# Four tiles' logits and gates turned by one transpose each, and bias products on bands of 32 rows

## The chip, the cores and the metric

The kernel runs on one core of one Trainium2 chip. The metric is the device time of one execution in microseconds (us), as the median over runs. The tensor engine is called PE, the vector engine DVE, the scalar engine ACT, GpSimd POOL, and the engine that issues most of the transfers SP.

## The reference

Two layers over `x` of 8 batches x 256 time steps x 256 channels. Layer 0 is a decayed scan followed by a mixture of eight gated experts with a router; layer 1 is a gated linear attention followed by a top-2 choice among eight 256x256 experts, with a bias for each. Two pieces matter here. Both routers multiply every token (row of x) by a 256x8 matrix to get eight logits for that token. And layer 1 adds, for every token, the two chosen experts' bias rows weighted by their gates:

```
logits = x @ gate_w.T                       # [tokens, 8]
gates  = softmax over the best two of 8
out    = sum over the two e: gates[e] * (x @ expert_w[e] + expert_b[e])
```

## The kernel before

The 2048 tokens are worked on in four groups (`GROUPS`) of 512, each of four tiles of 128 tokens (`TILES = 4`). Every matrix product is made in three passes of rounded operands (high by high, high by low, low by high; `passes`, L706). Group g's layer-1 work is laid between the layer-0 work of group g+1. Each engine runs a program of its own, in the order in which the functions are called in its `group` function; semaphores tie them together. The order of each engine is written out by hand.

**Logits.** `router_start` makes the logits of 512 tokens with the token along the free dimension: a PSUM bank of 16 rows (8 high parts, 8 low parts) by 512 columns. ACT (`logits_out`, L1078 is its copy helper) copies 16x512 to SBUF in one instruction, into `logitT`, a part of `weighted[1]`. `router_end` (L740 to L745) then turns it tile by tile: four transposes of 16x128, into 16 columns each. DVE reads the 64 columns (`route_start` for layer 0, `gates_start` for layer 1). There are two of these per group. On PE, layer 0's `router_end` stands right behind `transpose_y` of the group before, and layer 1's between the products r and k of `project_rkv`.

**Gates and bias.** `spread_gates` (DVE) writes the gates of a tile three times, at columns 0, 32 and 64 of 96 (`BIAS_K`), high and low parts. `transpose_gates` (L924) turns four tiles with four transposes of 128x96 into one bank; ACT (`gates_out`) copies 96x512 out as `gatesT`. `project_o` begins each tile's output product with `gatesT[:, cols]` times `bias_w` of 96 rows (L938) and goes on with six passes of the attention's output matrix in the same accumulation. In groups 0 to 2 its results lie two tiles to a bank (M0: tiles 0 and 1, M1: tiles 2 and 3), and DVE's `result` adds them to the rows two by two.

**Making bias_w.** SP loads the 8x256 bias three times into `bias_raw`, which POOL has cleared. POOL rounds it to `bias_w` (L574), subtracts for the low part (L577), then overwrites `bias_raw` with the two constant matrices `mean_w` and `ahead` (memset L580, affine_select L582) that PE's `rank` and `moments` use later. All of it stands ahead of POOL's group loop.

**Around it.** SP clears the DRAM tensor `sorted_rows` once, with nine long transfers from one zeroed row (L463). They are issued before anything of `store_part`. POOL's `scan_add(0)` scales the scan's output with gamma (L590) and adds it to the rows (L596), two tiles ready at a time (`scan_added`). DVE's `y_add` waits for these adds, then come `y_norm` and `y_out` (L1547), and PE's `transpose_y` (L830) waits for `y_out`.

Of the kernel before, what the change touches and what calls it, by code (L numbers as in the profile page):

```python
# [40 lines left out]
BIAS_ROWS = (0, 32, 64)  # L41
BIAS_K = 96
# [52 lines left out]
def build(nc, x, weights, lora_gu, lora_down, small, bias, gamma_row, beta_row, sorted_rows, returned, part, out):  # L95
    ctx = ExitStack()
    with ctx:
        def sb(name, shape, dt=F32):
            return ctx.enter_context(nc.sbuf_tensor(name, shape, dt))
# [25 lines left out]
        bias_w = sb("bias_w", [BIAS_K, D], F32R)  # L125
# [25 lines left out]
        gatesT = nc.alloc_sbuf_tensor_at("gatesT", [BIAS_K, GT], F32R, offset=r_at)  # L151
        gates_row = sb("gates_row", [P, TILES * BIAS_K])
        gates_wide = gates_row[:, :].rearrange("p (t c) -> p t c", t=TILES)
# [109 lines left out]
        bias_made = sem("bias_made")  # L263
        routers_ready = sem("routers_ready")
# [18 lines left out]
        logitT_ps = [sem(f"logitT_ps{n}") for n in range(2)]  # L283
        logitT_copied = [sem(f"logitT_copied{n}") for n in range(2)]
# [121 lines left out]
        def logitT(layer):  # L406
            return weighted[1][0:2 * E, 2 * layer:2 * layer + 2, 0:D]
# [23 lines left out]
        def _(sp):  # L431
# [91 lines left out]
        def _(pool):  # L523
# [4 lines left out]
            nc.gpsimd.memset(bias_raw[:, :], 0.0).then_inc(bias_made, 1)  # L528
# [38 lines left out]
            for t in range(TILES):  # L567
# [5 lines left out]
            pool.wait_ge(bias_loaded, 16 * 3)  # L573
            nc.gpsimd.tensor_copy(bias_w[:, :], bias_raw[0:BIAS_K, :]).then_inc(bias_made, 1)  # L574
            pool.wait_ge(bias_made, 2)
            row = BIAS_ROWS[1]
            nc.gpsimd.tensor_tensor(bias_w[row:row + E, :], bias_raw[row:row + E, :],  # L577
                                    bias_w[row:row + E, :].bitcast(F32), ALU.subtract).then_inc(bias_made, 1)
            pool.wait_ge(bias_made, 3)
            nc.gpsimd.memset(bias_raw[:, :], 1.0 / P).then_inc(bias_made, 1)  # L580
            pool.wait_ge(bias_made, 4)
# [1369 lines left out]
```

## Time and profile before

| | us |
|---|---|
| median of 3 runs | 430.26 |
| lowest, highest | 429.86, 434.49 |
| the profiled execution's own time | 429.93 |
| its span (first to last instruction) | 428.2 |
| PE busy | 421.4 (98%) |
| DVE busy | 344.0 (80%) |
| ACT busy | 179.9 (42%) |
| POOL busy | 170.9 (40%) |

The profiled execution took 1.73 us more than its span. The granted clock of PE is full in all forty slices. The transfers are dense in three stretches: up to about 32 us (weights), from about 43 to 91 us (the clearing of `sorted_rows`), and in the last third.

### The profile page before, as it was taken

To read this page: it belongs to the slowest core of one execution; us is meant where nothing else is said; L and a number is where in the kernel's file an instruction comes from. 1 tells how busy PE (TensorE), PEld (TensorE's weight loads), DVE (VectorE), ACT (ScalarE), POOL (GpSimd) and SP (SyncE) were. 2 spreads that over 40 slices of the span, in tenths; PEclk is the share of its full clock that TensorE was granted. 3 is DMA by queue.
4 is the path that set the end of the run, shared out by engine and by line. 5 is a ranking of instruction groups with operands and counts; after the bars stand their busy time and mean duration, and the time that the engine had idled before them with its cause. 6 is when DMAs were issued, how large, how long until landed. Compare 5 with 4: busy or idle time off the path is not lost.

```text
span 428.2 us, 7469 instructions
## 1 busy us (share of the span) xinstructions
PE 421.4 (98%) x2509; PEld 367.5 (86%) x2509; DVE 344.0 (80%) x1086; ACT 179.9 (42%) x337; POOL 170.9 (40%) x200
## 2 busy tenths in 40 slices
PE   7999999999999999999999999999999999999996
PEld 5788898887889998878888989788989889999886
DVE  6799996898898668989995798899978465856785
ACT  4745454432262736342446135423652333525130
POOL 1547369641036202500063806110531054655656
PEclk9999999999999999999999999999999999999999
DMA  8993899920002130000020400000111834521298
GB/s 273 368 325 132 260 301 294 299 57 0 2 25 75 51 99 2 0 0 2 2 98 7 139 5 0 2 0 2 61 39 48 245 127 124 173 88 61 101 233 259
DMA packets 30310, 46.89 MB, mean 110 GB/s; under 512 B 2696, under 2 KB 24480, under 8 KB 29760
## 3 DMA queue, kind: packets, MB, share of 16 engines
q1 hardware_dynamic: 25920, 35.75, 27.2%
q0 software_dynamic: 3360, 9.85, 7.9%
q10 hardware_dynamic: 992, 0.81, 0.6%
q8 instruction: 21, 0.34, 0.3%
q14 instruction: 17, 0.14, 0.1%
HBM read 22.74 MB, written 23.65 MB: 108 GB/s over the span
## 4 chain that ended last, share of the span: by engine, by line
PE 96%; DVE 2%; DMA 1%; issue 0%; DVEq 0%
PE D L706 29%; PE G L706 25%; PE U L706 25%; PE M L706 10%; PE D L735 1%; PE M L855 1%; PE M L830 1%; DMA rows<-x 1%; PE M L727 1%; PE D L742 0%; PE M L715 0%; PE M L938 0%; DVE stats L1375 0%; PE G L855 0%; PE M L924 0%
## 5 line engine op out<-in xcount | busy, mean ns | idle before, releaser
L706 PE MATMUL D<-w_hi,mid_hi 128*128 128x256 f32 x260 | 74.2, 285 | 0.1
L706 PE MATMUL D<-w_hi,mid_lo 128*128 128x256 f32 x260 | 73.6, 283 | 0.0
L706 PE MATMUL D<-w_lo,mid_hi 128*128 128x256 f32 x260 | 73.5, 283 | 0.0
L1109 ACT ACTIVATE mid<-G 128x512 f32<-128x512 f32 x64 | 38.0, 597 | 77.0 <-PE G L706 60.1
L1486 DVE TENSOR_TENSOR mid<-mid,U 128x512 f32<-128x512 f32 x64 | 43.2, 684 | 28.6 <-PE U L706 14.6
L549 POOL TENSOR_TENSOR w_lo<-w_raw,w_hi 128x512 fp32r<-128x512 f32 x35 | 49.9, 1453 | 23.4 <-ACT w_hi L1078 11.6
L1500 DVE SCALAR_TENSOR_TENSOR rows<-D,weight,rows 128x256 f32<-128x256 f32 x128 | 53.9, 476 | 4.3 <-PE D L706 4.1
L1365 DVE TENSOR_TENSOR mid_lo<-mid,mid_hi 128x512 fp32r<-128x512 f32 x64 | 50.4, 809 | 4.7 <-ACT mid_hi L1078 3.3
L1078 ACT ACTIVATE mid_hi<-mid 128x512 fp32r<-128x512 f32 x64 | 39.9, 630 | 32.2 <-DVE mid L1486 31.8
L706 PEld LDWEIGHTS D<-w_hi,mid_hi 128*128 128x128 f32 x260 | 49.8, 191 | 2.1 <-issue 1.4
L706 PE MATMUL G<-xT_hi,w_hi 128*128 128x512 f32 x126 | 50.3, 400 | 0.1
L706 PEld LDWEIGHTS D<-w_lo,mid_hi 128*128 128x128 f32 x260 | 49.8, 192 | 0.7
L706 PEld LDWEIGHTS D<-w_hi,mid_lo 128*128 128x128 f32 x260 | 49.8, 191 | 0.0
L706 PE MATMUL U<-xT_hi,w_hi 128*128 128x512 f32 x126 | 49.4, 392 | 0.0
L706 PE MATMUL G<-xT_lo,w_hi 128*128 128x512 f32 x126 | 49.3, 392 | 0.0
L706 PE MATMUL G<-xT_hi,w_lo 128*128 128x512 f32 x126 | 49.1, 390 | 0.0
L706 PE MATMUL U<-xT_hi,w_lo 128*128 128x512 f32 x126 | 49.1, 390 | 0.0
L706 PE MATMUL U<-xT_lo,w_hi 128*128 128x512 f32 x126 | 49.1, 389 | 0.0
L633 POOL DMA_INDIRECT sorted_rows<-weighted,slots x24 | 25.3, 1056 | 54.3 <-ACT weighted L1191 48.8
L590 POOL TENSOR_TENSOR scan_part<-scan_part,gamma 128x256 f32<-128x256 f32 x16 | 11.3, 737 | 60.7 <-ACT scan_part L1135 60.7
L706 PEld LDWEIGHTS G<-xT_hi,w_lo 128*128 128x128 f32 x126 | 23.7, 188 | 5.2
L706 PEld LDWEIGHTS U<-xT_hi,w_hi 128*128 128x128 f32 x126 | 23.7, 188 | 5.0
(368 smaller groups left out, 951.2 us busy)
## 6 DMA issues: line engine op xcount, KB each, us to landing
sorted_rows<-weighted SPq DMA_DIRECT2D x8, 1542.0 KB, 18.1
stage<-sorted_rows SPq DMA_DIRECT2D x31, 128.5 KB, 2.3
w_raw<-weights SPq DMA_DIRECT2D x2, 1280.0 KB, 16.2
w_raw<-weights SPq DMA_DIRECT2D x2, 1024.0 KB, 23.7
rows<-x SPq DMA_DIRECT2D x7, 256.0 KB, 3.0
w_raw<-weights SPq DMA_DIRECT2D x2, 768.0 KB, 9.2
part<-rows SPq DMA_DIRECT2D x12, 128.0 KB, 2.8
sums_gate<-part SPq DMA_DIRECT2D x3, 512.0 KB, 5.8
```

The costliest lines, as they stand in the source:

```text
L549: nc.gpsimd.tensor_tensor(flat, w_raw[:, n, :], w_hi[:, n, :, :].rearrange("p k d -> p (k d)").bitcast(F32), ALU.subtract).then_inc(pool_l ...
L590: nc.gpsimd.tensor_tensor(scan_part[:, t, :], scan_part[:, t, :], gamma[:, :], ALU.mult)\
L633: nc.gpsimd.indirect_dma_start(sorted_rows[:, :], bass.IndirectOffsetOnAxis(slots[:, q, j:j + 1], 0), weighted[j][:, t, :], None).then_inc ...
L706: ins = nc.tensor.matmul(out_ap, a, b, start=(first and n == 0), stop=(last and n == 3 * len(pairs) - 1))
L727: ins = nc.tensor.transpose(MT[k][:, t * P:(t + 1) * P], ln[:, t, k * P:(k + 1) * P], ident[:, :])
L735: ins = nc.tensor.matmul(bank[0:2 * E, :], routers[:, layer, k, :, :].rearrange("p a e -> p (a e)"), part[:, k, :], start=n == 0, stop=n = ...
L830: ins = nc.tensor.transpose(MT[k][:, t * P:(t + 1) * P], ln[:, t, k * P:(k + 1) * P], ident[:, :])
L1078: return nc.scalar.activation(o, i, ACT.Copy)
L1109: nc.scalar.activation(mid[:, c, :], GU[2 * c][:, :], ACT.Silu).then_inc(silu_ready, 1)
L1365: return v.tensor_tensor(o, i, hi.bitcast(F32), ALU.subtract)
L1486: v.tensor_tensor(mid[:, c, :], mid[:, c, :], GU[2 * c + 1][:, :], ALU.mult)\
L1500: ins = v.scalar_tensor_tensor(rows[g % 2][:, t, :], DN[t // 2][:, (t % 2) * D:(t % 2 + 1) * D], weight0[:, t, ORDER[e]:ORDER[e] + 1], row ...
```

## The change

The router's four 16x128 pieces are copied by four ACT instructions to the partitions 0, 32, 64 and 96 of one 128x128 square, and one 128x128 transpose turns them all. The gates of the four tiles are written side by side, 32 columns for a tile, so that one 128x128 transpose turns them. Tile t's transposed gates are then on partitions 32t to 32t+31, so `bias_w` is held four times, 32 rows each, and the bias product of tile t has 32 rows. In groups 0 to 2 the four outputs lie in alternate banks, PE waits for its own tile t-2 before tile t, and DVE's `result` waits for three tiles before its first add. The bias comes as one 128x256 load; low parts are made by POOL over all 128 rows in `bias_raw` and placed into `bias_w` by four SP transfers of 8 rows, issued behind the nine clearing transfers. The two constant matrices are made by POOL after these transfers have landed, inside `scan_add(0)`. DVE clears `weighted[1]` once at the start.

```diff
-BIAS_ROWS = (0, 32, 64)
-BIAS_K = 96
+BIAS_PARTS = 3
+BIAS_K = 32
-                return MT[t // 2][:, (t % 2) * D:(t % 2 + 1) * D]
+                return MT[t % 2][:, (t // 2) * D:(t // 2 + 1) * D]
         def logitT(layer):
-            return weighted[1][0:2 * E, 2 * layer:2 * layer + 2, 0:D]
+            return weighted[1][:, 2 * layer, 0:P]
-            sp.wait_ge(bias_made, 1)
-            for row in BIAS_ROWS:
-                sp.dma_start(bias_raw[row:row + E, :], bias[:, :]).then_inc(bias_loaded, 16)
+            sp.dma_start(bias_raw[:, :], bias[:, :]).then_inc(bias_loaded, 16)
...
                 sp.dma_start(empty, weighted[0][:, 0:1, :].broadcast_to([P, empty.shape[1], D + 1])).then_inc(cleared, 16)
+
+            sp.wait_ge(bias_made, 2)
+            for t in range(TILES):
+                rows_lo = slice(t * BIAS_K + E, t * BIAS_K + 2 * E)
+                sp.dma_start(bias_w[rows_lo, :].bitcast(F32), bias_raw[rows_lo, :]).then_inc(bias_placed, 16)
...
+            def make_means():
+                pool.wait_ge(bias_placed, 16 * TILES)
+                nc.gpsimd.memset(bias_raw[:, :], 1.0 / P).then_inc(bias_made, 1)
+                pool.wait_ge(bias_made, 3)
+                nc.gpsimd.affine_select(out=ahead, in_=ahead, compare_op=ALU.is_gt, fill=0.0, base=0, pattern=[[1, P]],
+                                        channel_multiplier=-1).then_inc(bias_made, 1)
...
             def scan_add(g):
...
                     nc.gpsimd.tensor_tensor(scan_part[:, t, :], scan_part[:, t, :], gamma[:, :], ALU.mult)\
                         .then_inc(scan_scaled, 1)
+                if g == 0:
+                    make_means()
                 for t in range(TILES):
...
             def router_end(bank, layer, g):
                 pe.wait_ge(logitT_copied[layer], g + 1)
-                for t in range(TILES):
-                    ins = nc.tensor.transpose(bank[:, t * 2 * E:(t + 1) * 2 * E],
-                                              logitT(layer)[:, t // 2, (t % 2) * P:(t % 2 + 1) * P],
-                                              ident[0:2 * E, 0:2 * E])
-                ins.then_inc(logit1_ps if layer else logit0_ps, 1)
+                nc.tensor.transpose(bank[:, 0:P], logitT(layer), ident[:, :])\
+                    .then_inc(logit1_ps if layer else logit0_ps, 1)
...
-                for t in range(TILES):
-                    ins = nc.tensor.transpose(late_banks(g)[0][0:BIAS_K, t * P:(t + 1) * P], gates_wide[:, t, :],
-                                              ident[:, :])
-                ins.then_inc(gatesT_ps, 1)
+                nc.tensor.transpose(late_banks(g)[0][:, 0:P], gates_wide, ident[:, :]).then_inc(gatesT_ps, 1)
...
-                    nc.tensor.matmul(o, gatesT[:, cols], bias_w[:, :], start=True, stop=False)
+                    if g < LAST and t >= 2:
+                        pe.wait_ge(proj_ps, at(g, TILES, t - 1))
+                    part = slice(t * BIAS_K, (t + 1) * BIAS_K)
+                    nc.tensor.matmul(o, gatesT[part, :], bias_w[part, :], start=True, stop=False)
...
-                copy(logitT(layer), halves_of(bank[0:2 * E, :])).then_inc(logitT_copied[layer], 1)
+                for t in range(TILES):
+                    ins = copy(logitT(layer)[32 * t:32 * t + 2 * E, :], bank[0:2 * E, t * P:(t + 1) * P])
+                ins.then_inc(logitT_copied[layer], 1)
...
-                    if g == LAST or t % 2 == 0:
-                        dve.wait_ge(proj_ps, at(g, TILES, t + 1 if g == LAST else t + 2))
+                    if g == LAST or t < 2:
+                        dve.wait_ge(proj_ps, at(g, TILES, t + 1 if g == LAST else t + 3))
...
+            v.memset(weighted[1][:, :, 0:P], 0.0).then_inc(logitT_cleared, 1)
```

## Rows read from the trace of the kernel before

**Rows 1.** The page's busy times, then the chain that ended last (start, us, what).
```profile
PE 421.4 (98%) x2509; PEld 367.5 (86%) x2509; DVE 344.0 (80%) x1086; ACT 179.9 (42%) x337; POOL 170.9 (40%) x200
...
81.70 2.87 PE D L706 x24
...
102.19 1.36 PE G L706 x6
```

**Rows 2.** Waits of PE: who waited for whom, us in total, times, longest.
```profile
PE M L945 <- DVE xT_lo L1765: 1.5, 1, 1.5
```

**Rows 3.** PE around layer 1's router_end: its durations, then the timeline (start, us, instruction).
```profile
L742 PE MATMUL D<-ident,weighted x24: 207/210/231, 94.6 to 277.8; 16*128 16x16 f32 x24
...
98.50 0.39 PE L706 MATMUL G<-yT_hi,w_lo 128*128 128x512 f32 x1
98.82 0.42 PE L742 MATMUL D<-ident,weighted 16*128 16x16 f32 x4
...
99.50 0.39 PE L706 MATMUL U<-yT_lo,w_hi 128*128 128x512 f32 x1
```

**Rows 4.** Timeline of PE around transpose_gates of group 0.
```profile
140.22 0.28 PE L706 MATMUL D<-w_hi,mid_lo 128*128 128x256 f32 x1
140.34 0.60 PE L924 MATMUL M<-ident,gates_row 128*96 128x128 f32 x4
...
141.01 0.39 PE L706 MATMUL G<-xT_lo,w_hi 128*128 128x512 f32 x1
```

**Rows 5.** Timeline of PE at the first bias product of project_o.
```profile
146.25 0.28 PE L938 MATMUL M<-bias_w,gatesT 96*128 96x256 f32 x1
146.37 0.28 PE L706 MATMUL M<-w_hi,yT_hi 128*128 128x256 f32 x1
```

**Rows 6.** Timeline of PE around the LoRA products of 64 rows.
```profile
40.86 0.39 PE L706 MATMUL U<-xT_hi,w_lo 128*128 128x512 f32 x1
41.18 1.99 PE L715 MATMUL M<-down_factors 64*128 64x256 f32 x8
...
43.32 0.28 PE L706 MATMUL D<-w_lo,mid_hi 128*128 128x256 f32 x1
```

**Rows 7.** Timeline of POOL before and in scan_add of group 0.
```profile
77.54 0.31 POOL L580 MEMSET bias_raw<- 128x256 f32 x1
77.93 0.31 POOL L582 TENSOR_SCALAR_AFFINE_SELECT bias_raw<-bias_raw 128x128 f32<-128x128 f32 x1
80.20 2.84 POOL L590 TENSOR_TENSOR scan_part<-scan_part,gamma 128x256 f32<-128x256 f32 x4 [1.96 <-ACT scan_part L1135]
...
84.95 3.14 POOL L596 TENSOR_TENSOR rows<-rows,scan_part 128x256 f32<-128x256 f32 x4 [1.91 <-DVE rows L1500]
```

**Rows 8.** SP's last clearing transfer; then transfers: KB each, us from issue to landing.
```profile
77.33 5.68 SPq L463 DMA_DIRECT2D sorted_rows<-weighted  x1
...
down_factors<-lora_down SPq DMA_DIRECT2D x1, 256.0 KB, 11.4
...
sorted_rows<-weighted SPq DMA_DIRECT2D x1, 128.5 KB, 13.4
```

**Rows 9.** Timeline of DVE and PE from y_add to transpose_y of group 0.
```profile
87.30 0.87 DVE L1500 SCALAR_TENSOR_TENSOR rows<-D,weight,rows 128x256 f32<-128x256 f32 x2
...
92.76 1.38 DVE L1547 TENSOR_SCALAR ln<-rows,mv,rstd 128x256 f32<-128x256 f32 x4
...
93.50 1.14 PE L830 MATMUL M<-ident,ln 128*128 128x128 f32 x8
```

**Rows 10.** Timeline of ACT: the logits copy, and an instruction of 32 columns.
```profile
97.54 0.59 ACT L1078 ACTIVATE weighted<-D 16x512 f32<-16x512 f32 x1 [0.38 <-PE D L735]
...
16.64 0.23 ACT L1123 ACTIVATE th<-logit 128x32 f32<-128x32 f32 x1 [0.49 <-DVE logit L1428]
```

**Rows 11.** Timeline of the first microseconds: PE's warm-up and DVE's first wait.
```profile
1.53 4.21 PE L945 MATMUL M<-xT_lo 128*128 128x512 f32 x9 [1.53 <-DVE xT_lo L1765]
...
4.33 1.41 DVE L1375 BATCH_NORM_STATS2 stats<-rows 128x6 f32<-128x256 f32 x4 [2.55 <-DMA rows<-x]
```

More of the change, by code:

```diff
@@ L40 @@
 JOBS = PAIRS * TILES
-BIAS_ROWS = (0, 32, 64)
-BIAS_K = 96
+BIAS_PARTS = 3
+BIAS_K = 32
+assert BIAS_K * TILES == P
 LN_EPS = 1e-5
@@ L124, in build @@
         expert_id = sb("expert_id", [P, E])
-        bias_w = sb("bias_w", [BIAS_K, D], F32R)
+        bias_w = sb("bias_w", [P, D], F32R)
         bias_raw = sb("bias_raw", [P, D])
@@ L263, in build @@
         bias_made = sem("bias_made")
+        bias_placed = sem("bias_placed")
         routers_ready = sem("routers_ready")
@@ L406, in logitT, with logit_parts @@
         def logitT(layer):
-            return weighted[1][0:2 * E, 2 * layer:2 * layer + 2, 0:D]
+            return weighted[1][:, 2 * layer, 0:P]
+        def logit_parts(bank):
+            return bank[:, 0:P].rearrange("p (t c) -> p t c", t=TILES)[:, :, 0:2 * E]
         def logit0_bank(g):
@@ L527, in _ @@
             nc.gpsimd.memset(carry_gain[:, 0, :], 0.0).then_inc(const_made, 1)
-            nc.gpsimd.memset(bias_raw[:, :], 0.0).then_inc(bias_made, 1)
             pool.wait_ge(const_made, 3)
@@ L572, in _ @@
             split_low(17, WHERE["o"])
[L573 to L581, printed above, removed]
-            nc.gpsimd.affine_select(out=ahead, in_=ahead, compare_op=ALU.is_gt, fill=0.0, base=0, pattern=[[1, P]],
-                                    channel_multiplier=-1).then_inc(bias_made, 1)
+            pool.wait_ge(bias_loaded, 16)
+            nc.gpsimd.tensor_copy(bias_w[:, :], bias_raw[:, :]).then_inc(bias_made, 1)
+            pool.wait_ge(bias_made, 1)
+            nc.gpsimd.tensor_tensor(bias_raw[:, :].bitcast(F32R), bias_raw[:, :], bias_w[:, :].bitcast(F32),
+                                    ALU.subtract).then_inc(bias_made, 1)
+            def make_means():
[4 more added lines that the diff above has]
+                                        channel_multiplier=-1).then_inc(bias_made, 1)
             def scan_add(g):
@@ L839, in rank @@
             def rank(g):
[L840 removed]
+                pe.wait_ge(bias_made, 4)
                 pe.wait_ge(chosen_step, at(g, TILES + 1, TILES + 1))
@@ L1118, in logits_out @@
                 bank = logit1_bank(g) if layer else logit0_bank(g)
-                copy(logitT(layer), halves_of(bank[0:2 * E, :])).then_inc(logitT_copied[layer], 1)
+                if g == 0 and layer == 0:
+                    act.wait_ge(logitT_cleared, 1)
+                for t in range(TILES):
+                    ins = copy(logitT(layer)[32 * t:32 * t + 2 * E, :], bank[0:2 * E, t * P:(t + 1) * P])
+                ins.then_inc(logitT_copied[layer], 1)
             def route_start(g):
@@ L1196, in gates_out @@
                 act.wait_ge(gatesT_ps, at(g, 1, 1))
-                copy(gatesT[:, :], late_banks(g)[0][0:BIAS_K, :]).then_inc(gatesT_ready, 1)
+                copy(gatesT[:, :], late_banks(g)[0][:, 0:P]).then_inc(gatesT_ready, 1)
             def att_norm(g, c):
@@ L1556, in gates_start @@
                 dve.wait_ge(logit1_ps, at(g, 1, 1))
-                back(v.tensor_copy(halves[:, :, :, :].rearrange("p t a e -> p (t a e)"),
-                                   logit1_bank(g)[:, 0:TILES * 2 * E]))
+                back(v.tensor_copy(halves[:, :, :, :].rearrange("p t a e -> p t (a e)"),
+                                   logit_parts(logit1_bank(g))))
                 v.tensor_tensor(logit1[:, :, :], halves[:, :, 0, :], halves[:, :, 1, :], ALU.add)\
@@ L1633, in spread_gates @@
                 back(v.memset(gates_wide, 0.0))
-                parts = gates_wide.rearrange("p t (n c) -> p t n c", n=len(BIAS_ROWS))[:, :, :, 0:E]
-                for n in range(3):
+                parts = gates_wide.rearrange("p (t n c) -> p t n c", t=TILES, c=E)
+                for n in range(BIAS_PARTS):
                     ins = v.tensor_copy(parts[:, :, n, :].bitcast(F32R), gates[:, :, :])
@@ L1935 @@
         "small": small,
-        "bias": a(L1_ffn_expert_b),
+        "bias": np.tile(np.concatenate([a(L1_ffn_expert_b)] * BIAS_PARTS
+                                       + [np.zeros((BIAS_K - BIAS_PARTS * E, D), np.float32)]), (TILES, 1)),
         "gamma_row": a(L0_attn_gamma).reshape(1, D),
```

12 lines of the change are left out of this document (6 added, 6 removed).

## The prediction

> **What bounds the kernel now.** I read the page first: PE is busy 98% of a span of 428.2 us, the chain that ended last is PE nearly throughout, and its stretches follow each other without a hole [rows 1]. Then PE's waits: the longest of all is 1.5 us, before the first instruction, and the others come to 1.5 us together [rows 2]. So from some 15 us on PE's own stream sets the time. A microsecond taken off PE is a microsecond gained, one put on it is lost, and work on the other engines counts only where PE comes to wait for it. Then the timeline of PE, for what one slot costs: six products of 512 columns in 1.36 us are 0.23 us each, 24 of 256 columns in 2.87 us are 0.12 us each [rows 1]. The price of a small block is the time between the starts of two big products on its two sides, less their own slots. Last the timeline of POOL, SP and DVE from 77 to 94 us, where the change puts a new chain of waits.
>
> **Transposes of the gates.** From the start of the last product before to the start of the second one after are 141.01 - 140.22 = 0.79 us [rows 4]; without the block it would be 0.12 + 0.23 = 0.35. Four transposes cost 0.44 us, 0.11 each. One is left: 0.33 saved in each of four groups, **-1.3 us**. Its 128 columns against 96 I take at nothing; a transpose of 128x128 at L830 runs at a similar pace, eight in 1.14 us [rows 9]. If the wider load cost in proportion it would be 0.03 us. ACT's copy of the gates and DVE's memset get shorter, off the path.
>
> **Transposes of the logits.** 99.50 - 98.50 = 1.00 us, less 2 x 0.23, is 0.54 us for four transposes of 16 rows [rows 3]. That is more than four full ones cost. Four starts at 16 columns take 0.42 - 0.21 = 0.21 us for three gaps [rows 3], 0.07 each, 0.28 for four; so 0.26 us of the 0.54 is not the transposes but going in and out. The new one has 128 rows: 0.11 us. Saved are 0.43 us each time, eight times, the last group's taken alike: **-3.4 us**.
>
> **The bias product.** With 96 rows it costs a plain slot, 146.37 - 146.25 = 0.12 us, with nothing at its edges [rows 5]. With 32 rows it is of the kind of the 16-row and 64-row blocks, and both have edges. The 64-row block: 43.32 - 40.86 = 2.46, less 0.35 is 2.11 us, against 1.99 us from the first start to the last end [rows 6], so at least 0.12 us of edge; counting that the last one's end reaches beyond its slot, as at L742, it is nearer 0.27. I take 0.27 us for an in-and-out, between 0 (as 96 rows) and 0.54 (as the whole 16-row block). Before, one edge pair was shared by four transposes; now every bias product stands alone between full-height ones, 16 in all: **+4.3 us** (0 to 8.6). The Trainium skill speaks against the change here: TensorEngine Tiling, Key Properties, says that a change of tiling mode, not of tile, drains the engine, and that modes are by 128, 64 or 32 rows. By that rule 32 rows switch and 96 do not; the trace agrees, with 0.26 us at the edges of 16 rows and none at 96. By the other reading of the same page, that small tiles run beside others, the product would cost less than its slot, at best 16 x 0.12 = 1.9 us gained.
>
> **PE's wait for its own tile t-2** is hidden: a product ends 0.28 us after its start [rows 5], and tile t-1's seven slots, 0.84 us, lie between. Without that cover it would cost up to 0.28 us, six times. DVE's `result` starts one tile later and has three adds left once the fourth tile is done; PE needs them only after 24 slots, 2.87 us, of `down`. Nothing.
>
> **The four logit copies.** One copy of 512 columns takes 0.59 us, an instruction of 32 columns 0.23 [rows 10]; 128 columns are about 0.3 and, pipelined, four about 0.9 (bounds 0.59 and 4 x 0.59 = 2.36). The copy for layer 1 is then done at 97.54 + 0.9 = 98.4; PE wants it at 98.50 + 0.23 = 98.7 [rows 3]. Nothing, with 0.3 us to spare; at the upper bound 1.2 us in each of three groups, 3.5 us. Behind it on ACT stands `mid_high`, which waits for DVE anyway. Layer 0's copy has more room, with eight y transposes before it is wanted.
>
> **The start.** DVE's memset of 512 columns (half a microsecond, like the one before the warm-up) falls into its 2.55 us idle before 4.33 [rows 11]. One SP issue instead of three, 128 KB instead of 24, POOL's memset gone: PE is not waiting for any of it later. Nothing.
>
> **The chain through SP and POOL.** This one is not hidden. The low parts of the bias go out on SP behind nine clearing transfers. The last of these is being issued from 77.33 to 83.01 and lands 13.4 us after 77.33, at 90.7 [rows 8]. The four new transfers are issued from 83.0 on, on the same queue. That a transfer waits behind older ones there shows at `down_factors`: 256 KB landing after 11.4 us [rows 8], for which `rows` needed 3.0 later. So I have them land at 90.5, between 88 and 91.5, as the tail of the clears thins out. At the lowest, were they to pass the clears, they land after 86.
>
> POOL has scaled its four tiles by 83.04 [rows 7]. In the kernel before it starts to add at 84.95; now it stands in `make_means` until 90.5. Then memset and affine_select, 77.54 to 78.24 before, 0.7 us; then the adds, 3.14 / 4 = 0.79 us each, two of them for `scan_added` [rows 7]: 90.5 + 0.7 + 1.57 = 92.8. Queued behind it on POOL are `add_beta` and the counting, which are not due. DVE's `y_add` waits for that sum, and began at 87.30 [rows 9]: 5.5 us late. Everything to `y_out` hangs on it, so `y_out` starts at 92.76 + 5.5 = 98.3. PE began `transpose_y` at 93.50, with the first tile ready at 92.76 + 0.4 [rows 9]: it had 0.2 to 0.3 us to spare. PE is delayed by **5.3 us**, part of it at `router_start` (which waits for the first half of `y_add`), the rest at `transpose_y`. The first group's one saved logits block before this place, 0.43 us, is swallowed by the wait, so seven of eight count.
>
> **The sum.** 5.3 - 7 x 0.43 (3.0) - 1.3 + 4.3 = +5.3 us. Span 433.5, plus the 1.73 us outside the span: 435.2 us. The profiled execution was at 429.93, 0.33 us below the median of 430.26; I leave the forecast at 435.2, the two being within the scatter.
>
> **Rivals.**
> 1. *The stall, but no edges at 32 rows*: the 96-row product speaks for it, the 16-row and 64-row ones against. 435.2 - 4.3 = 430.9. Chance 0.17.
> 2. *The edges, but no stall*: the four transfers land before 85.2 or so, since they are small and pass the clears. `down_factors` speaks against. 429.9 - 3.4 - 1.3 + 4.3 = 429.5. Chance 0.10.
> 3. *The change does what it says*, the other sign: one mechanism, that PE's stream is shorter by 4.7 us with nothing given back; 425.2. It takes both a landing before 85.2 and no edges. It decides, as faster, from a sum below -4.3. Chance 0.05.
> 4. *The stall also costs the clock.* PE stands still twice for about 2.7 us. At the start, after standing still, nine products of 512 columns take 4.21 us, about 0.45 each, against 0.23 later [rows 1, 11]: that is the pace of 1.2 GHz, though the granted clock of these slices reads full. Nine such slots again would be 9 x 0.22 = 2.0 us more: 437.2. For it: two waits close together; against: each is short and work lies between. Chance 0.10. TensorE: Matmul & The Clock Gate, Part 1, in the Trainium skill also has an idle array return to 1.2 GHz.
>
> The forecast itself: 0.58, with a range of its own of 433.3 to 436.8 (landing 89 to 91.5, edge 0.2 to 0.3 us).
>
> **How the numbers follow.** The range from 429.3 to 437.3 leaves out rival 3 and the outer ends. Faster by over 1% (below 426.0): 0.05. Slower by over 1% (above 434.6; one per cent is about what a measurement tells from no change): the upper two thirds of the forecast, rival 4, and a little more, 0.50. Within 1%: 0.45.
>
> **What would show it.** The chain of waits in the changed kernel should have POOL idle ahead of its memset of `bias_raw` for 7 us until a transfer into `bias_w` lands near 90.5, and PE idle twice near 91 and 96 us, 5 us together. The starts of PE around a bias product of 32 rows should lie about 0.4 us apart (0.12 + 0.27) instead of 0.12. A logits block should go from 0.54 to 0.11 us, the gates block from 0.44 to 0.11. If the bias product keeps its plain slot, rival 1 holds; if POOL does not wait, rival 2. ACT's four copies taking more than 1.2 us together would break the step that has them hidden.

## The result, and the profile after

| | before | changed |
|---|---|---|
| median, us (5 executions each, side by side) | 429.89 | 440.06 |
| lowest, highest | 429.86, 434.49 | 438.28, 442.87 |
| the profiled execution | 429.93 | 438.28 |
| its span | 428.2 | 436.5 |

The ratio is 1.0216, with a 95% interval from 1.017 to 1.0263: slower, by about 9 us; that it is slower is clear, whether by more than 2% the interval leaves open. The forecast was 435.2 us and its range ended at 437.3, below even the fastest execution, 438.28.

Executions of nearly every kernel here, of before too, come at two levels some 4.3 us apart, a difference that arises in the first 17 us, where TensorE in some executions keeps the pace of 1.2 GHz longer (last section); so below I compare executions of the lower level, which for the pair above are 429.9 and 438.3 to 438.7, **+8.4 us** from fastest to fastest.

The page of the changed kernel, its busy times, the granted clock in 40 slices, and the shares of the chain that ended last:

```profile
PE 425.5 (97%) x2473; PEld 365.8 (84%) x2473; DVE 344.1 (79%) x1087; ACT 182.4 (42%) x361; POOL 170.0 (39%) x199
...
PEclk9999999989999999999999999999999999999999
...
PE 76%; SPq 10%; DVE 9%; DMA 2%; issue 2%; ACT 1%; POOL 0%; POOLq 0%; DVEq 0%; ACTq 0%
```

PE's share of the chain, nearly the whole of it before [rows 1], is 76% now: at one place the chain leaves PE and runs back through DVE and POOL into SP's queue. One slice no longer reads 9 in the clock. The waits of PE (total, times, longest), where before had one long one and 1.5 us of others [rows 2]:

```profile
PE D L746 <- DVE rows L1512: 2.6, 1, 2.6
...
PE M L838 <- DVE ln L1559: 1.2, 1, 1.2
PE D L717 <- DVE mid_lo L1377: 0.9, 1, 0.9
```

These three are new. To see where the first two come from, the chain in order of time from SP's last clear on (start, us, what):

```profile
78.23 5.43 SPq L467
...
83.70 0.77 SPq L472
...
85.90 5.28 DMA bias_w<-bias_raw
...
91.23 0.31 POOL bias_raw L589
...
93.31 0.89 DVE rows L1512 x2
```

The four small transfers are issued from 83.70, behind the clears. The last one's issue starts at 85.90 and it has landed 5.28 us later, at 91.18, right behind the last clear (issued from 78.23, landed 12.8 us later, at 91.0); POOL starts `make_means` at 91.23. The timelines of POOL and DVE say the same from the side of those who wait (start, us, instruction, idle before it and its releaser):

```profile
80.48 2.83 POOL L599 TENSOR_TENSOR scan_part<-scan_part,gamma 128x256 f32<-128x256 f32 x4 [2.56 <-ACT scan_part L1147]
91.23 0.31 POOL L589 MEMSET bias_raw<- 128x256 f32 x1 [7.92 <-DMA bias_w<-bias_raw]
...
93.31 0.88 DVE L1512 SCALAR_TENSOR_TENSOR rows<-D,weight,rows 128x256 f32<-128x256 f32 x2 [5.64 <-POOL rows L607]
...
99.05 1.38 DVE L1559 TENSOR_SCALAR ln<-rows,mv,rstd 128x256 f32<-128x256 f32 x4
```

Against [rows 9] `y_add` starts 93.31 - 87.30 = 6.0 us late and `y_out` 99.05 - 92.76 = 6.3. On PE:

```profile
91.25 0.39 PE L717 MATMUL U<-xT_hi,w_lo 128*128 128x512 f32 x1
94.25 0.85 PE L746 MATMUL D<-xT_hi,routers 128*16 128x512 f32 x2 [2.61 <-DVE rows L1512]
...
96.17 0.63 PE L717 MATMUL G<-xT_lo,w_hi 128*128 128x512 f32 x1
96.60 0.63 PE L717 MATMUL G<-xT_hi,w_lo 128*128 128x512 f32 x1
...
99.52 1.41 PE L838 MATMUL M<-ident,ln 128*128 128x128 f32 x8 [1.23 <-DVE ln L1559]
```

`transpose_y` starts at 99.52 instead of 93.50: +6.0. Between the two waits the G products stand 96.60 - 96.17 = 0.43 us apart instead of 0.23, the pace of 1.2 GHz. Windows of 1 us confirm it (stretch: its length, PE busy and instructions, granted clock, share of the transfers, GB/s):

```profile
95.00:96.00 1.00, 1.00 (x4) 0.50 0.00 0
...
98.00:99.00 1.00, 0.29 (x2) 1.00 0.00 0
```

The granted clock fell after PE had stood still for 2.6 us and was full again from 98 us on.

Then the three kinds of small block, which stand all over the kernel. A bias product (to be held against [rows 5]):

```profile
151.28 0.39 PE L717 MATMUL U<-xT_hi,w_lo 128*128 128x512 f32 x1
151.59 0.38 PE L946 MATMUL M<-bias_w,gatesT 32*128 32x256 f32 x1
151.90 0.39 PE L717 MATMUL M<-w_hi,yT_hi 128*128 128x256 f32 x1
152.13 0.28 PE L717 MATMUL M<-w_lo,yT_hi 128*128 128x256 f32 x1
...
152.81 0.38 PE L946 MATMUL M<-bias_w,gatesT 32*128 32x256 f32 x1
```

From one bias product to the next are 1.22 us. Seven plain slots would be 0.84; the edges of one 32-row product are **0.38 us**. One can see how they are made: 0.08 us more before it (151.59 - 151.28 = 0.31 for a slot of 0.23), 0.19 behind it, and the product after starts slowly as well (0.39 long, the next 0.23 later, where a plain slot is 0.12). The weight loads (PEld) show what is lost. In the kernel before (first row below) the load for the 96-row product starts 0.22 us ahead of the product (146.25, [rows 5]), under the product before it. In the changed kernel the load for the 32-row product starts only with the product itself, and the load for the wide product behind it only with that one:

```profile
146.03 0.19 PEld L938 LDWEIGHTS M<-bias_w,gatesT 96*128 96x128 f32 x1
...
151.59 0.18 PEld L946 LDWEIGHTS M<-bias_w,gatesT 32*128 32x128 f32 x1 [0.35 <-issue]
151.90 0.19 PEld L717 LDWEIGHTS M<-w_hi,yT_hi 128*128 128x128 f32 x1
```

The gates block (against [rows 4]):

```profile
145.79 0.28 PE L717 MATMUL D<-w_hi,mid_lo 128*128 128x256 f32 x1
145.91 0.27 PE L931 MATMUL M<-ident,gates_row 128*128 128x128 f32 x1
...
146.25 0.39 PE L717 MATMUL G<-xT_lo,w_hi 128*128 128x512 f32 x1
```

146.25 - 145.79 = 0.46, less 0.35, is 0.11 us, where it was 0.44. A logits block (against [rows 3]):

```profile
104.45 0.39 PE L717 MATMUL G<-yT_hi,w_lo 128*128 128x512 f32 x1
104.68 0.31 PE L752 MATMUL D<-ident,weighted 128*128 128x128 f32 x1
...
105.06 0.40 PE L717 MATMUL U<-yT_lo,w_hi 128*128 128x512 f32 x1
```

105.06 - 104.45 = 0.61, less 0.46, is 0.15 us, where it was 0.54: 0.39 saved.

Then the third new wait in the list. Early in group 0 ACT's four copies of 16x128 take 1.08 us (one of 16x512 took 0.57), and DVE's work behind them comes later; PE's first `down` product waits for `mid_lo`:

```profile
14.09 1.08 ACT L1086 ACTIVATE weighted<-M 16x128 f32<-16x128 f32 x4
...
24.61 0.36 PE L717 MATMUL D<-w_hi,mid_hi 128*128 128x256 f32 x1 [0.86 <-DVE mid_lo L1377]
```

In the kernel before that product starts at 24.15, so PE is 0.46 us late there, though it had come to the place 0.4 us early.

**Where the 8.3 us of span went, by places on PE's timeline.** At 24.6 us: +0.46. At the second U product behind `transpose_y` of group 0 (101.10 against 95.25): +5.85, which holds all before it, since PE waited. (`transpose_y` itself starts 6.02 us late; the logits block right behind it takes 0.34 us less than before, but the eight transposes ahead of it 0.17 us more.) Behind that place stand six logits blocks (-0.39 each, -2.3), four gates blocks (-0.33, -1.3) and sixteen bias products (+0.38, +6.1): +2.4. Together 8.3 (5.85 and 2.4), and the span is 8.3 us longer. In every full group the drift is 4 x 0.38 - 0.33 - 2 x 0.39 = +0.41; read at the first `down` block of three groups in a row the lag is 6.76, 7.22 and 7.67 us, so +0.45.

### The profile page after: what moved, and what is told of

It reads as the page before. It is cut to its first block, busy times and chain, and to the rows that moved or that the text cites. A ratio compares the mean times of both kernels' runs of the same rounds, so it can differ in the third digit from the quotient of the medians.

```text
span 436.5 us, 7423 instructions
## 1 busy us (share of the span) xinstructions
PE 425.5 (97%) x2473; PEld 365.8 (84%) x2473; DVE 344.1 (79%) x1087; ACT 182.4 (42%) x361; POOL 170.0 (39%) x199
## 4 chain that ended last, share of the span: by engine, by line
PE 76%; SPq 10%; DVE 9%; DMA 2%; issue 2%; ACT 1%; POOL 0%; POOLq 0%; DVEq 0%; ACTq 0%
PE D L717 23%; PE U L717 19%; PE G L717 19%; SPq L467 9%; PE M L717 9%; DMA bias_w<-bias_raw 1%; PE D L746 1%; DVE rows L1512 1%; PE M L946 1%; PE M L838 1%; PE M L863 1%; DVE carry_gain L1736 1%; DMA rows<-x 1%; DVE mid L1498 1%; DVE gamma L1738 1%
## 5 line engine op out<-in xcount | busy, mean ns | idle before, releaser
L717 PEld LDWEIGHTS G<-xT_hi,w_hi 128*128 128x128 f32 x126 | 24.1, 191 | 4.6 <-issue 0.3
```

Source lines behind the costliest of these rows:

```text
L717: ins = nc.tensor.matmul(out_ap, a, b, start=(first and n == 0), stop=(last and n == 3 * len(pairs) - 1))
```

## The experiments

Twelve runs were made, one of them the changed kernel again, on four chips. The chips are not alike (at its lower level before takes some 430 us on the first and third, 438.6 and 437.3 on the other two), so each time is held against before, or another kernel, on its own chip.

### First set: each part alone

**The logits part alone**, in the kernel before: its `logitT`, `router_end`, four ACT copies and DVE's reading as in the change, the gates, the bias and SP's order as before.

```diff
-                for t in range(TILES):
-                    ins = nc.tensor.transpose(bank[:, t * 2 * E:(t + 1) * 2 * E],
-                                              logitT(layer)[:, t // 2, (t % 2) * P:(t % 2 + 1) * P],
-                                              ident[0:2 * E, 0:2 * E])
-                ins.then_inc(logit1_ps if layer else logit0_ps, 1)
+                nc.tensor.transpose(bank[:, 0:P], logitT(layer), ident[:, :])\
+                    .then_inc(logit1_ps if layer else logit0_ps, 1)
```

> The kernel before with the logits part alone: four ACT copies to bands of 32 partitions and one 128x128 transpose, eight times; gates, bias products and their set-up as before. Theory: each block costs 0.15 us instead of 0.54, as in the changed kernel's trace, so 7 x 0.39 = 2.7 us are gained on PE; the first block's gain is lost and 0.45 us more, because the four copies at 14 us push ACT and DVE back, which PE then waits for at its first down product. Sum -2.3 us, 427.6 us. Rival (the logits part is what costs, through the four ACT copies): 430 us or more.

Measured: 427.57, 427.79, 427.94 and 428.07 us at the lower level (median of all ten 431.19; ratio 0.9965, 0.9916 to 1.0015) against 430.07 for before. **-2.2 us.** Eight blocks at 0.39 would be 3.1; the start takes back the first one's saving and 0.46 us besides (the same wait for `mid_lo` at 24 us is in this trace): 7 x 0.39 - 0.46 = 2.3. The gain rests on comparing the lower level: six of the ten executions lie at 430.8 us or above, and the interval of the ratio includes 1, no change.

**The wait gone, the 32 rows kept.** The low parts go to a buffer of their own, so nothing waits for the transfers before `bias_raw` is overwritten:

```diff
-            nc.gpsimd.tensor_tensor(bias_raw[:, :].bitcast(F32R), bias_raw[:, :], bias_w[:, :].bitcast(F32),
+            nc.gpsimd.tensor_tensor(bias_low.bitcast(F32R), bias_raw[:, :], bias_w[:, :].bitcast(F32),
...
-                pool.wait_ge(bias_placed, 16 * TILES)
+                pool.wait_ge(bias_made, 2)
...
-                sp.dma_start(bias_w[rows_lo, :].bitcast(F32), bias_raw[rows_lo, :]).then_inc(bias_placed, 16)
+                sp.dma_start(bias_w[rows_lo, :].bitcast(F32), bias_low[rows_lo, :]).then_inc(bias_placed, 16)
```

`bias_low` is a free part of `weighted[1]`; PE's `project_o` and ACT's first `weigh` wait for `bias_placed` instead, long after it has come.

> The changed kernel with one wait taken out: the low parts of the bias are staged in a free part of weighted[1] instead of in bias_raw, so POOL may overwrite bias_raw at once and scan_add(0) no longer waits for the four transfers; PE waits for them only before project_o. Theory: the delay of 5.5 us at the first group's end goes, and with it the scatter over executions that comes from when the clearing ends: 432.7 us against 438.3 of the changed kernel's profiled run, executions within 1 us of each other. Rival (the wait is hidden anyway, the loss is in PE's products): 438 to 440 us and the same scatter.

Measured: 432.01 to 432.38 us in nine of ten executions (median 432.16, ratio 1.003, 0.9986 to 1.0073). Its POOL:

```profile
83.16 0.31 POOL L591 MEMSET bias_raw<- 128x256 f32 x1
83.55 0.82 POOL L593 TENSOR_SCALAR_AFFINE_SELECT bias_raw<-bias_raw 128x128 f32<-128x128 f32 x1
85.15 1.05 POOL L609 TENSOR_TENSOR rows<-rows,scan_part 128x256 f32<-128x256 f32 x1 [0.79 <-DVE rows L1516]
```

POOL makes the means at 83.16 and is ready to add before DVE is: both waits of PE are gone. So is the scatter, of which more below.

**The wait kept, the 32 rows gone.** The bias product takes all 128 rows (its sum is then over four tiles' gates, not one tile's: the output isn't the reference's).

```diff
-                    nc.tensor.matmul(o, gatesT[part, :], bias_w[part, :], start=True, stop=False)
+                    nc.tensor.matmul(o, gatesT[:, :], bias_w[:, :], start=True, stop=False)
```

> The changed kernel with its bias products over all 128 rows instead of a band of 32, so every tile adds the bias rows of all four tiles' gates (left out: the choice of the tile's own band). The wait behind the clearing stays. Theory: the edges go: a bias product costs 0.12 us instead of 0.50, 16 x 0.38 = 6.1 us less, 432 us in a run like the profiled one, and the scatter over executions stays. Rival (32 rows cost nothing; the rest is the wait alone): 438 us, no change.

Measured: 432.01, 432.44, 432.47, 432.8, 432.89, 433.32, 434.07 and 434.61 at the lower level (median of all ten 433.1; ratio 1.0046, 1.0 to 1.0093). The spread from 432.0 to 434.6 is back with the wait.

**Both undone**: the two diffs before this one together (the output as in the last).

> Both of the two edits above: low parts staged elsewhere and bias products over all 128 rows (left out: the choice of the tile's own band). Theory: what is left of the change is the gain of the one transpose for logits and gates, 2.7 + 1.3 us, less 0.45 us at the start: 426.4 us, and little scatter. If the two causes overlap, the sum of the two single gains is more than this one; if a third cause exists, it stays above 428 us.

Measured, as expected: eight of ten between 425.95 and 426.52, median 426.49 us; ratio 0.9894, 0.9846 to 0.9942.

The four corners answer the question of size twice each:

| | with the wait | without | the wait costs |
|---|---|---|---|
| 32 rows | 438.3 (the changed kernel) | 432.1 | 6.2 |
| 128 rows | 432.5 | 426.5 | 6.0 |
| the 32 rows cost | 5.8 | 5.6 | |

For 128 rows with the wait I take 432.5, between the lowest execution (432.0) and the middle of the eight (432.85), so each difference holds to about half a microsecond. The corner of the changed kernel stems from another chip, with before at 429.9 against 430.1. What stays when both are undone is 430.1 - 426.5 = 3.6 us, the gain of the transposes. 6.1 + 5.7 - 3.6 = 8.2: the parts add up to the 8.4 measured, within that half microsecond, and none hides in another.

### Second set: what an edge depends on, and what the transfers wait for

On this chip executions of before with a full clock take 438.3 to 438.8 us at the lowest level (median of all 25: 440.29); in twelve of the 25 the mean granted clock is 0.988 to 0.996, though nothing is changed in them, and PE has some waits in the last third that it has not on the first.

**Before with 32 of its 96 rows** in the bias product (the parts with the other rows are left out of the sum).

```diff
-                    nc.tensor.matmul(o, gatesT[:, cols], bias_w[:, :], start=True, stop=False)
+                    nc.tensor.matmul(o, gatesT[0:32, cols], bias_w[0:32, :], start=True, stop=False)
```

> The kernel before with its bias products cut to the first 32 of 96 rows (left out: the low parts of bias and gates); nothing else is changed. Theory: the height of 32 rows by itself costs what the changed kernel's trace shows, 0.50 us a product instead of 0.12, 16 x 0.35 to 0.38 = 5.7 to 6.1 us: 435.9 us in executions like the 430.1 us ones of before. Rival (the edges come from the bands at partitions 32, 64, 96, or from the wait for the own tile t-2): 430.1 us.

Measured: 443.27, 443.7 and 443.73 us for the lowest (median 444.12, ratio 1.0105, 1.0063 to 1.0148), some **5 us** more from this one line, a little under the 5.7 to 6.1 expected; this chip's own waits may take up the rest, which isn't shown. Its PE:

```profile
146.15 0.38 PE L938 MATMUL M<-bias_w,gatesT 32*128 32x256 f32 x1
...
147.37 0.38 PE L938 MATMUL M<-bias_w,gatesT 32*128 32x256 f32 x1
```

The pitch is 1.22 us again. Here the tiles' results lie as before, PE has no wait for its own tile t-2, and all four products use the same band. So neither the changed banks, nor that wait, nor the wandering from band to band make the edge.

**The same with `gatesT[0:64, cols]` and `bias_w[0:64, :]`**, one execution.

> The kernel before with its bias products cut to 64 of 96 rows (left out: the low parts of the gates). Theory, that every height other than the full array's pays the edges: a product costs 0.50 us as with 32 rows. Rival, that the cost grows as the rows get fewer: between 0.12 and 0.50 us.

Measured: 444.81 us, and

```profile
146.65 0.38 PE L938 MATMUL M<-bias_w,gatesT 64*128 64x256 f32 x1
...
147.87 0.38 PE L938 MATMUL M<-bias_w,gatesT 64*128 64x256 f32 x1
```

the pitch is 1.22 us once more. 64 rows cost what 32 cost, 96 cost nothing [rows 5].

**Two bias products back to back**, those of tiles 0 and 1 and of 2 and 3, on the kernel without the wait.

```diff
+                def bias_part(t):
...
+                    part = slice(t * BIAS_K, (t + 1) * BIAS_K)
+                    nc.tensor.matmul(proj_at(g, t), gatesT[part, :], bias_w[part, :], start=True, stop=False)
+
                 for t in range(TILES):
...
+                    if t % 2 == 0:
+                        bias_part(t)
+                        bias_part(t + 1)
```

> The kernel with the staging buffer (432.1 us), bias products of two tiles issued one behind the other, then both tiles' other products. Theory, that the cost is one of going into and out of the 32-row shape: a pair shares the edges, eight in-and-outs instead of 16, 8 x 0.35 = 2.8 us less, 429.3 us. Rival, that every product of 32 rows costs it by itself: 432.1 us, unchanged.

Measured: 436.55 us with a full clock, seven more from 436.7 to 438.2 (median 437.12, ratio 0.9932, 0.9888 to 0.9975). Below before by about 1.9 us; the kernel without pairs, +2.05 on the first chip, should be near 440.6 here (an estimate; it did not run on this chip), so pairing brings 3 to 4 us, more than the 2.8 expected. The reason:

```profile
147.27 0.28 PE L719 MATMUL M<-w_hi,yT_lo 128*128 128x256 f32 x1
147.48 0.38 PE L948 MATMUL M<-bias_w,gatesT 32*128 32x256 f32 x2
147.79 0.39 PE L719 MATMUL M<-w_hi,yT_hi 128*128 128x256 f32 x1
148.01 0.28 PE L719 MATMUL M<-w_lo,yT_hi 128*128 128x256 f32 x1
```

148.01 - 147.27 = 0.74, less two plain slots, is 0.50 us for *two* bias products, and a single one in the changed kernel costs the same 0.50 (0.12 and its edges). The pair, on different partitions and into different banks, takes the time of one.

**The four transfers on ACT's queue** instead of behind SP's clears, POOL's wait as in the change:

```diff
+            def scan_norm(g):
+                if g == 0:
+                    act.wait_ge(bias_made, 2)
+                    for t in range(TILES):
...
+                        act.dma_start(bias_w[rows_lo, :].bitcast(F32), bias_raw[rows_lo, :]).then_inc(bias_placed, 16)
```

> The changed kernel with the four small transfers issued by ACT on its own queue, at its first idle place after the low parts are made, about 78 us, instead of by SP behind the clearing transfers. Everything waits for them as before. Theory, that they are late because they stand behind the clears in SP's queue: they land by 82 us, POOL does not wait, 432.1 us as with the staging buffer. Rival, that they are late because the same 16 DMA engines are full until 90 us: they land at 86 us or later and 2 us or more of the delay stays, 434 us or more.

Measured: 441.46, 442.11 and 442.63 us for the lowest (median 444.79, ratio 1.0077, 1.0034 to 1.012). ACT and POOL:

```profile
77.98 3.23 ACTq L1144 DMA_DIRECT2D bias_w<-bias_raw  x4
...
81.96 2.83 POOL L594 TENSOR_TENSOR scan_part<-scan_part,gamma 128x256 f32<-128x256 f32 x4 [4.01 <-ACT scan_part L1147]
86.64 0.31 POOL L584 MEMSET bias_raw<- 128x256 f32 x1 [1.85 <-DMA bias_w<-bias_raw]
```

Mixed. At a full clock the fastest is 442.11, 3.8 us above before, where the theory had 2.0 and the rival 3.9 or more. POOL restarts at 86.64 instead of 91.23, so most of the stall was the place in SP's order. But POOL goes on only 5.4 us after the last of the transfers, 8 KB each and alone on their queue, was issued (81.2); behind the clears it was 4.7 us (issued by 86.5, POOL at 91.23). The DMA engines' share in windows of 2 us was 1.09 up to 86 us and 0.82 up to 88, nearly all of it clears. A queue of its own let the transfers land before the clears were through (their share is still 0.27 from 88 to 90 us), but it did not spare them the load. And issuing took ACT 3.2 us, for which the scan had to wait (81.96 instead of 80.48).

### Third set: is there a version that beats both?

**Block-diagonal gates.** One transpose for the gates, as in the change; ACT copies each tile's 32 rows to its own 128 columns of a `gatesT` of 128x512, which POOL has cleared; the bias product takes 128 rows, so the zeros take the place of the band. The low parts have their own buffer, and the outputs lie two tiles to a bank as before, without PE's wait for its own tile. The result is the reference's whole computation.

```diff
-                copy(gatesT[:, :], late_banks(g)[0][:, 0:P]).then_inc(gatesT_ready, 1)
+                for t in range(TILES):
+                    part = slice(t * BIAS_K, (t + 1) * BIAS_K)
+                    ins = copy(gatesT[part, t * P:(t + 1) * P], late_banks(g)[0][part, 0:P])
...
-                    nc.tensor.matmul(o, gatesT[part, :], bias_w[part, :], start=True, stop=False)
+                    nc.tensor.matmul(o, gatesT[:, cols], bias_w[:, :], start=True, stop=False)
```

> The changed kernel without its two losses and with the full result: low parts staged apart, and each tile's 32 transposed gate rows copied by ACT into its own 128 columns of a 128x512 square that POOL has cleared, so that the bias product can run over all 128 rows of bias_w, where the other tiles' rows meet zeros. Theory: the one transpose for gates and logits is kept, products cost 0.12 us, POOL's memset and ACT's four copies are hidden: 426.5 us, as with both losses undone. Rival: ACT's four copies or POOL's memset come late for project_o or for the next group, 428 us or more.

Measured: 426.38, 426.44, 426.5 us and one at 430.3, against 429.94 and 430.09; median 426.47, ratio 0.9883, 0.9799 to 0.9966. **It beats both kernels**, before by 3.6 us at the lower level (four executions, so the size is less sure than the sign), and loses nothing against the kernel with both parts undone (426.5).

**The same with the first logits block done the old way**: one copy of 16x512 by ACT and four transposes of 16 rows by PE where `g == 0 and layer == 0`, as in the kernel before.

> The same, and the very first block of logits turned in the old way (one ACT copy of 512 columns, four transposes of 16 rows). Theory: there the four copies push back ACT and DVE, for which PE waits 0.86 us at its first down product; without them 0.46 us come back: 426.0 us. Rival (the PE wait has another cause): 426.5 us, unchanged.

Measured: 425.82, 425.95, 426.34 and 426.44 at the lower level (ratio 0.9844, 0.9774 to 0.9914), 0.3 us less than the one before where 0.46 was expected. The wait for `mid_lo` is gone from its list of PE's waits; the gain itself is at the edge of what these few executions can tell.

### Fourth set: does the stall cost clock?

**PE kept busy in its two gaps**: ten products of 512 columns, whose results nobody reads, ahead of `router_start`, ten ahead of `transpose_y`, in group 0 alone.

```diff
+                    def keep_busy(q):
+                        for _ in range(10 if g == 0 else 0):
+                            nc.tensor.matmul(GU[q][:, :], w_at(w_hi, "gate0", 0, slice(0, P)), xT_hi[:, 0, :],
+                                             start=True, stop=True)
+
+                    keep_busy(2)
                     pe.wait_ge(down_added, at(g, 2 * E, 2 * E - 1))
...
-                    gate_up(nxt, 0, [1], between=lambda: [transpose_y(g), router_end(D0, 0, nxt)])
+                    gate_up(nxt, 0, [1], between=lambda: [keep_busy(3), transpose_y(g), router_end(D0, 0, nxt)])
```

> The changed kernel, with ten products of 512 columns (whose results are never read) put into each of PE's two gaps: ahead of router_start and ahead of transpose_y in group 0. At 0.23 us each they take 2.3 us and end before what PE waits for (the gaps are 2.6 us, and 2.7 us when the products between them are at full pace). Theory: standing still costs nothing but the wait itself, since in the profiled execution the second wait took up what the lower clock between 94 and 98 us cost; the fastest executions stay where those of the changed kernel are (438.3 on the earlier chip, 8.3 us above the kernel before), and only the granted clock (0.995 there) reads full. Rival (part of the 8.3 us, and the executions near 440, are the clock): 0.9 to 1.8 us less than the changed kernel run beside it, and a G product is 0.23 instead of 0.43 us after the one before.

**The changed kernel again**, beside it.

> The changed kernel unaltered, for its times on the same chip as the one with filled gaps: about 8.3 us above the kernel before. If the clock in the wait is what sets some executions 1.8 us above the fastest, these show a granted clock of 0.99 or less in most executions while the kernel with filled gaps does not; otherwise both have them alike.

Measured, in the order they ran, with the mean granted clock of each (before on this chip: 437.34 at the lowest, clock 1.0). The changed kernel's ratio to before is 1.0221 (1.0153 to 1.029), as in the first pair; with filled gaps it is 1.016 (1.01 to 1.022):

| | us (clock) |
|---|---|
| filled gaps | 446.53 (.996), 448.21 (.992), 446.37 (.996), 447.9 (.996), 445.24 (1.0), 445.72 (.996) |
| changed kernel | 448.05 (.996), 450.86 (.996), 450.24 (.996), 449.96 (.996), 450.84 (.996), 445.01 (1.0) |

Neither expectation came out whole. The two fastest, both at a full clock, are alike, 445.24 and 445.01, 7.7 to 7.9 us above before: the fills themselves cost nothing, and most of the loss is there without any loss of clock. But the profiled executions differ where the stall ends. The changed kernel here:

```profile
100.29 1.97 PE L838 MATMUL M<-ident,ln 128*128 128x128 f32 x8 [2.83 <-DVE ln L1559]
...
105.26 0.39 PE L717 MATMUL G<-yT_hi,w_hi 128*128 128x512 f32 x1
```

and with filled gaps:

```profile
97.12 2.43 PE L1034 MATMUL U<-xT_hi,w_hi 128*128 128x512 f32 x10
100.11 1.40 PE L838 MATMUL M<-ident,ln 128*128 128x128 f32 x8 [0.57 <-DVE ln L1565]
...
103.89 0.40 PE L717 MATMUL G<-yT_hi,w_hi 128*128 128x512 f32 x1
```

The same work takes 105.26 - 100.29 = 4.97 us in the one and 103.89 - 100.11 = 3.78 in the other; in the profiled execution ahead of the experiments it took 3.78 too. In that one the clock had fallen between the two waits, and the second wait took the loss up; here it stayed full behind the first, of 3.3 us, and fell to 0.50 behind the second (windows 101 to 103 us), and nothing takes it up: **1.2 us**. The trace of the kernel with 128 rows is of the second kind: waits of 2.3 and 2.8 us, and 0.50 behind the second, from 104 to 106 us. With filled gaps every window from 91 to 106 us reads 1.00. So in these traces the stall costs clock, and whether that costs time hangs on which of the two waits it falls behind. With the gaps filled it costs none at that place, in the one trace that there is.

The means of this chip can't say how often: the filled kernel's is 0.996 too, from a stretch between 380 and 400 us (0.91 there). Those of the first chip can: 0.988 to 0.996 in all ten executions with the stall and 128 rows, 0.999 or 1.0 in all twenty of the two kernels without the stall. The rest of the 3.65 us between the two medians (446.45 and 450.1) I can't place: this chip's own waits come in, and six executions over two levels are few.

## Why the prediction was wrong

The forecast had the mechanisms and their places, and was 3.1 us short of the executions of its own kind (435.2 against 438.3), 4.9 short of the median. Of the 3.1, 1.8 are the edges, 0.7 the stall and 0.5 the logits. Term by term:

**The bias product's edges: the step that failed, by size.** Forecast +4.3 (16 x 0.27), the trace of after says 16 x 0.38 = +6.1, the corners of the first set 5.6 to 5.8. The 0.27 was taken from blocks: the 16-row transposes (0.26 for going in and out) and eight 64-row products [rows 6]. The misreading is in the second. I subtracted 1.99 us, the time from the first start to the last *end*, and put back for the end that reaches beyond its slot only what the 16-row transposes showed, some 0.15 us. The block's own durations (in ns) and its first and last start give more:

```profile
L715 PE MATMUL M<-down_factors x8: 376/376/480, 41.2 to 42.8; 64*128 64x256 f32 x8
```

A product there is 0.38 us long, so the last one starts at 41.18 + 1.99 - 0.38 = 42.79 and reaches 0.26 beyond a slot of 0.12: 0.12 + 0.26 = 0.38 us of edges. Or by starts alone: of the 2.11 us, 1.61 lie between the first and the last start, and the 0.50 left are one product with its edges, exactly what a single one costs in the changed kernel. So the true price stood in the trace of before, in the very rows that the forecast used. They show one thing more: the eight starts are 0.23 us apart, so a row of 64-row products on one band costs nearly twice the plain slot for each, besides the edges.

The rule that a change of tiling mode drains the array (the Trainium skill, TensorEngine Tiling (Array Packing), Key Properties) fits what 32, 64 and 96 rows did here (edges, edges, none); the page names no price. The other rule there, that tiles run side by side, holds as well, but it needs two narrow products next to each other, as the paired kernel has and the changed one hasn't.

**The chain through SP and POOL: right, and 0.5 to 0.7 us too small.** Landing was put at 90.5 and was 91.18, POOL's restart at 91.23; DVE's `y_add` 6.0 us late, not 5.5; PE at `transpose_y` 6.0, not 5.3. The transfers did wait behind the clears, as the forecast had from `down_factors` [rows 8]: they landed right behind the last clear, and on ACT's queue before it. The forecast had them land 0.2 us ahead of the last clear (90.5 against 90.7); they came 0.15 us behind it. The corners put the wait's whole cost at 6.0 to 6.2.

**The four ACT copies and the start: "nothing" was wrong for the first of eight.** For layer 1 the copies were hidden, as reckoned. But they took 1.08 us against 0.57, and at the start nothing covers them: +0.46 us at 24 us and the first block's 0.4 lost. In the sum that is swallowed by the stall, since PE waits there anyway; without the stall it is real (-2.2 us for the logits part alone instead of -3.1). The sign I had named, that four copies take more than 1.2 us, did not show (1.08), and the step failed all the same: the forecast took for granted that layer 0 had more room than layer 1. It has in groups 1 to 3, not in group 0. That the copies are the cause is shown by the last kernel of the third set, in which that wait is gone.

**The transposes: right.** The gates block 0.44 to 0.11, as forecast. The logits block 0.54 to 0.15 instead of 0.11, so 0.39 saved and not 0.43. Of the seven blocks that I counted, the one right behind `transpose_y` brought 0.34, but the eight transposes ahead of it took 0.17 us longer, so 0.17 is left; with six at 0.39 that is -2.5 and not -3.0.

**PE's wait for its own tile: nothing, as forecast**; the pitch is 1.22 us with it and without it.

**The clock (rival 4): right in kind, and the reason for part of the distance to the median.** It was given one chance in ten because the waits were short with work between. The clock fell all the same. In 28 of the 31 executions of before on the first chip it reads 1.0, as it does with both parts undone; in the kernels with the whole stall (the changed one, the one with 128 rows) it read 0.988 to 0.996, but for one execution. The price was put at 2.0 us, for nine slots; in the traces it was 0 where the second wait took it up and 1.2 where it didn't. The 440.06 of the median has the lowest clock of its five, 0.988: that this is the clock falling behind both waits is likely, and not shown.

The same sum with the measured terms: 6.0 at `transpose_y`, -2.5, -1.3, +6.1 = +8.3, and 429.9 + 8.3 = 438.2. The range was too narrow at the top because of the edge as well. It ended at 437.3, next to rival 4's 437.2, and the forecast's own part of it at 436.8, with the landing at 91.5 and the edge at 0.30. An edge of 0.38 lies beyond that, though inside the 0.54 that the forecast itself had as the bound of an edge.

## What to carry to other kernels

A lone product of 256 columns and 32 or 64 rows among full-height ones cost four times its plain slot here (0.50 us against 0.12); where rows are to be picked, put zeros beside them and stay at full height, or lay the narrow products next to each other on different partitions. A small transfer on which an engine waits must not be issued behind bulk on the same queue, and on another queue it still shares busy DMA engines; give its source a buffer that nobody overwrites, and the wait is gone. Where an edge is to be priced and only a block is in the trace, count from start to start, down to the last start in the block; the end of a record reaches beyond its slot, and a sum that subtracts up to it hides that much of the edge.

## What was new of the hardware

- A single product of 256 columns costs 0.50 us at 32 rows and at 64, 0.12 at 96 and at 128. Of these four heights two pay the whole price and two none; what lies between 64 and 96 did not run. Its weights are not loaded under the product before it, nor those of the next wide product under it.
- Two products of 32 rows on different bands, into different banks, start together and cost 0.50 us together.
- PE's granted clock went to 0.50, 1.2 GHz, behind a wait of 2.6 us in one trace; in two others it stayed full behind a first wait of 3.3 and 2.3 us and fell behind a second of 2.8. The length of one wait alone does not tell. The Trainium skill (TensorE: Matmul & The Clock Gate, Part 1) has an idle array go back to this level; these falls agree with it.
- The two levels 4.3 us apart come from the start. In an execution of the upper level (that of the kernel with 128 rows) the router's products at 16.73 us take 1.05 us for two and `router_end` comes at 19.56; in one of the lower level (the changed kernel's) they take 0.62 and it comes at 15.22. That is 4.3 us, and it stays to the end. The granted clock reads 1.00 there in both, so it is the pace of the products that tells, 0.43 us from one start to the next against 0.23. What decides between them is open.
